# Where ScalarE copies the transposed rows of the second normalisation, and three waits at the end of an attention stage

## What is computed

```python
x = x + tanh(g_xattn[0]) * xattn(layernorm(x), ctx, ctx, mask, Wq, bq, Wk, bk, Wv, bv)
x = x + tanh(g_ffn[0]) * ffn(layernorm(x), Wg, W1, W2, W3)

# xattn: softmax over the 128 keys of the sequence
scores = einsum('bqhd,bkhd->bhqk', Qh, Kh) / sqrt(10.0)
scores = where(mask == 0, -1e9, scores)
out = einsum('bhqk,bkhd->bqhd', softmax(scores), Vh)

# ffn: every expert takes its top tokens
scores = (x_flat @ Wg.T).T
top_vals, token_idx = top_k(scores, capacity)
h = silu(xg @ W1.T) * (xg @ W3.T)
y = (h @ W2.T) * softmax(top_vals)[..., None]
out = zeros.at[token_idx].add(y)
```

## Time and profile before

| | us |
|---|---|
| median of 3 runs | 866.33 (866.3 to 868.46) |
| profiled execution, its own time | 867.74 |
| its span, first to last instruction | 866.0 |
| PE busy | 756.6 (87%) |
| DVE busy | 564.3 (65%) |
| ACT busy | 512.4 (59%) |
| POOL busy | 370.4 (43%) |

### The profile page before, as it was taken

How to read it: one execution, slowest core, us unless ns; L and a number is a source line. 1 busy time by engine, 2 the same in 40 slices (tenths; PEclk the granted TensorE clock), 3 DMA queues, 4 the chain that set the end, 5 groups by cost and what they waited for, 6 DMA issues and landing times. The chain is left out here.

```text
span 866.0 us, 24846 instructions
## 1 busy us (share of the span) xinstructions
PE 756.6 (87%) x9570; PEld 633.0 (73%) x9570; DVE 564.3 (65%) x1436; ACT 512.4 (59%) x1001; POOL 370.4 (43%) x777
## 2 busy tenths in 40 slices
PE   1599999999999999999998841599999999999993
PEld 1477878777877778777876720379888888988983
DVE  3367877777777777777776689755746556474440
ACT  3236676767766776677765757265555655556641
POOL 6232444424452435343522230435484654747505
PEclk9779999999999999999999975599999999999997
DMA  4243345335433544355312235135364453624314
GB/s 133 88 137 121 113 157 164 106 124 174 163 120 119 165 163 131 108 164 164 127 64 91 78 97 174 50 123 117 95 109 117 81 112 71 131 46 86 37 13 49
DMA packets 76773, 97.07 MB, mean 112 GB/s; under 512 B 8264, under 2 KB 55880, under 8 KB 76616
## 3 DMA queue, kind: packets, MB, share of 16 engines
q1 hardware_dynamic: 64368, 78.44, 28.2%
q0 software_dynamic: 12288, 17.05, 12.1%
HBM read 52.37 MB, written 25.72 MB: 90 GB/s over the span
## 5 line engine op out<-in xcount | busy, mean ns | idle before, releaser
L725 DVE TENSOR_REDUCE m_sb<-a_ps 128x4 f32<-128x512 f32 x256 | 164.7, 685 | 69.4 <-PE a_ps L1017 60.0
L559 ACT ACTIVATE p_t<-b_ps 128x512 f32<-128x512 f32 x252 | 141.6, 589 | 84.5 <-PE b_ps L1025 82.1
L1017 PE MATMUL a_ps<-k_st,q_st 31*128 31x128 f32 x2048 | 152.2, 287 | 10.6 <-DMA q_st<-q_val 5.9
L1017 PEld LDWEIGHTS a_ps<-k_st,q_st 31*128 31x128 f32 x2048 | 128.0, 190 | 36.3 <-issue 31.8
L1411 POOL DMA_INDIRECT out<-y,idx_add x64 | 100.3, 1567 | 110.7 <-ACT y L1470 100.0
L1025 PE MATMUL b_ps<-q_st,k_st 32*128 32x128 f32 x1984 | 144.4, 283 | 0.0
L475 POOL TENSOR_TENSOR x<-o_n,x_res 128x256 f32<-128x256 f32 x63 | 46.1, 731 | 208.2 <-DVE o_n L814 176.1
L1025 PEld LDWEIGHTS b_ps<-q_st,k_st 32*128 32x128 f32 x1984 | 120.7, 187 | 0.0
L1792 PE MATMUL bank<-x_hi,w_hi 128*128 128x512 f32 x254 | 100.0, 394 | 0.0
L1657 DVE TENSOR_TENSOR act_h<-act_h,bank 128x512 f32<-128x512 f32 x64 | 44.0, 688 | 84.4 <-PE bank L1792 78.3
L1792 PE MATMUL bank<-x_lo,w_hi 128*128 128x512 f32 x254 | 99.0, 390 | 0.0
(11 more groups left out here) (283 smaller groups left out, 1726.2 us busy)
## 6 DMA issues: line engine op xcount, KB each, us to landing
w<-in_w_t SPq DMA_DIRECT2D x24, 512.0 KB
rows_scratch<-xg SPq DMA_DIRECT2D x16, 528.0 KB, 3.5
x_in<-in_x SPq DMA_DIRECT2D x16, 512.0 KB, 4.7
c_t<-in_ctx_t SPq DMA_DIRECT2D x16, 512.0 KB, 4.6
k_st<-k_val SPq DMA_DIRECT2D x64, 128.0 KB
q_st<-q_val SPq DMA_DIRECT2D x64, 128.0 KB, 2.4
x_res<-in_x SPq DMA_DIRECT2D x16, 512.0 KB, 3.8
out<-x SPq DMA_DIRECT2D x16, 512.0 KB, 3.2
```

The source lines that it names most:

```text
L559: act.activation(p_t[b.s % 2][:, 4 * r:4 * r + 4, :], ps[q % 2][:].rearrange("p (h s) -> p h s", s=P), ACT.Exp, scale=SCALE).then_inc(exp_ ...
L725: dve.tensor_reduce(m_sb[b.s % 2][:, 4 * q:4 * q + 4], a_ps[q % 2][:].rearrange("p (h s) -> p h s", s=P), AX_X, ALU.max).then_inc(max_done, 1)
L1017: mm = pe.matmul(a_ps[i][:, t * P:(t + 1) * P], q_st[p][r:r + A_K, t, tok], k_st[p][r:r + A_K, t, tok], start=True, stop=True)
```

## The change

In ScalarE's `step` the copy `xt2_copy` moves ahead of the two first exponentials and the negated maximum. At the attention's end four things are done. PE's `values` of the last batch, which writes `f_ps`, no longer waits for ScalarE's copy out of `pv_ps` (`pv_out`) but for the second copy of transposed rows (`xt2_out`), which is the last reader of `f_ps`. `scores_back` moves ahead of `out_back(NB - 3)` and `values(NB - 2)` on PE. On VectorE `fold_last(1)` moves behind the division of batch NB-3, and the statistics of batches NB-3 and NB-2 change places with divisions. The scaled output of the last batch gets a tile of its own, `o_n_last`, so that it need not wait until GpSimd has read `o_n`.

```diff
+    o_n_last = sb("o_n_last", [P, D])
...
             def step(act, b):
                 g, f = b.group, b.group.on(1)
+                if b.j < 2:
+                    xt2_copy(g.on(-3), b.j)
                 exp(b.back(2), 0)
                 negate(b.back(1))
                 exp(b.back(2), 1)
-                if b.j < 2:
-                    xt2_copy(g.on(-3), b.j)
...
-            def scale_out(b, ps=o_ps):
+            def scale_out(b, ps=o_ps, to=o_n):
...
-                wait(dve, x2_done, b.times(1))
+                if to is o_n:
+                    wait(dve, x2_done, b.times(1))
...
-                dve.tensor_tensor(o_n[:].rearrange("p (h d) -> p h d", d=DH), o[:, :, 0:DH],
+                dve.tensor_tensor(to[:].rearrange("p (h d) -> p h d", d=DH), o[:, :, 0:DH],
...
             row_scores(group(NG - 3))
-            fold_last(1)
             divide(batch(NB - 3))
             scale_out(batch(NB - 3))
+            fold_last(1)
+            row_stats(batch(NB - 3))
             divide(batch(NB - 2))
-            row_stats(batch(NB - 3))
             scale_out(batch(NB - 2))
             divide(batch(NB - 1), b_ps[0])
+            scale_out(batch(NB - 1), b_ps[0], o_n_last)
             row_stats(batch(NB - 2))
-            scale_out(batch(NB - 1), b_ps[0])
             add_last()
...
-                    wait(pe, pv_out, b.times(1))
+                    if ps is pv_ps:
+                        wait(pe, pv_out, b.times(1))
+                    else:
+                        pe.wait_ge(xt2_out, back.times(2, 2))
...
+            scores_back(group(NG - 3), edge)
             out_back(batch(NB - 3))
             for q in range(4):
                 values(batch(NB - 2), q, group(NG - 3))
-            scores_back(group(NG - 3), edge)
             for q in range(4):
                 values(batch(NB - 1), q, group(NG - 3), f_ps)
```

More of the change, by code:

```diff
@@ L892, in add_last @@
                 dve.wait_ge(s_res[1], b.group.turn(16, 16))
-                dve.tensor_tensor(x2[1][:, b.j, :], o_n[:], x_res[1][:, b.j, :], ALU.add).then_inc(x2_done, 1)
+                dve.tensor_tensor(x2[1][:, b.j, :], o_n_last[:], x_res[1][:, b.j, :], ALU.add).then_inc(x2_done, 1)
             def last_scales():
```

## The result

The changed kernel takes 842.23 us (median of 4 runs, 841.49 to 843.42) where the kernel before takes 866.32. The ratio is 0.9717, with a 95% interval of 0.9698 to 0.9737. The profiled execution has its own time of 842.56 us and a span of 840.8 us; the forecast was 841.6 us and a span of 841.3.

A forecast was written before the change was run, and what follows sets the result against it. PE was taken to bound the kernel, busy 756.6 of 866.0 us, idling 20.5 us for ScalarE's copy. Gains of 18.5 + 4.5 + 1.7 = 24.7 us off 866.33 gave 841.6 us, range 839.5 to 846.5.

The forecast's parts named there:

- The steady groups: Twelve groups with copies: PE's wait ahead of values goes, 1.24 us in j=0 and 0.30 in j=1, 18.5 us in all.
- The cover: ScalarE ahead of the first exponential: the copy fits in idle time, with 0.53 us left in j=0.
- The margin at the step's end: End of steady step j=0: PE stays last, 0.16 us behind VectorE's chain (6.32 against 6.16 us).
- Rival (b): Steady step j=0: VectorE or ScalarE takes PE's place, 4.9 us lost, 846.5 us; chance 0.12.
- The last group: Final group with copies: two steps fall to 5.15 and 5.3 us, gaining 4.5 us, with PE's clock fall gone.
- rival (a): Final group with copies and attention's end give less, only 3.3 and 0.75 us: 843.8 us; chance 0.14.
- The end: Attention's end: three waits or delays on the chain to last_scales go, 1.7 us in all.
- PE's 0.75: Attention's end: values of the last batch starts earlier, no longer waiting for ScalarE's o_t, gaining 0.75 us.
- VectorE's two: Attention's end: statistics leave the way between division and scaling, 0.5 us; the wait for GpSimd's addition goes, 0.48 us.
- VectorE would wait for POOL nowhere: Attention's end, sign in the changed profile: VectorE has no wait for GpSimd (POOL).
- (c): PE ahead of values: the wait only changes its name, such as to the batch's exponentials; 860 us, chance 0.04.
- (d): Denser PE gets a lower clock: 7% lost eats the 24.7 us, 8% gives 871 us; chance 0.02.

The follow-up runs named there:

- second-place kernel: The changed kernel with ScalarE's copy one place further back, between the first exponential and the negated maximum; 851.87 us, ratio 0.9811.
- runs with more copies: The changed kernel with added ScalarE copies behind the moved one: 128x512, 128x1024 or both; 842.8, 843.2 and 850.1 us.
- kernel with the old last group: The changed kernel with ScalarE's copy back behind the exponentials in the final group that has copies only; 847.6 us, ratio 0.9769.
- PE's end alone: The changed kernel with VectorE's order and single o_n at the attention's end put back, PE's edits kept; 843.39 us in one execution.
- VectorE's end alone: The changed kernel with PE's edits at the attention's end put back, VectorE's edits kept; 845.9 us in one execution.
- the move alone: The kernel before with only ScalarE's copy moved ahead of the exponentials, nothing done at the attention's end; 844.39 us, ratio 0.974.

## Why the prediction was right

**The steady groups.** Predicted 12 x 1.54 = 18.5 us, measured 18.8. The step lengths were forecast as 6.32 and 7.42 us and came out as 6.32 and 7.39. What carried this was the group without copies, which runs the same steps with the same partners: it showed both where `values` can start and what would be last if it did. The second-place kernel shows the cause itself.

**The cover.** The copy was taken to lie in ScalarE's idle time with 0.53 us left; 0.60 us were. The margin at the step's end was given as 0.16 us and measured as 0.15. Rival (b) was priced at 0.41 us a step for a push of 0.57; the runs with more copies pay 0.05 for 0.21 and 0.57 for 0.72, the same line. Its mechanism was named too narrowly: PE's wait for the second exponential comes at the same delay as VectorE's chain, and PE meets it first.

**The last group.** Predicted 5.15 and 5.3 us, measured 5.11 and 5.29, and the gain of 4.5 us came out as 4.5. The step behind that number is sound only in part. The gain consists of 3.1 us that are always there (6.54 + 7.00 - 5.11 - 5.29) and of a fall of the clock, which cost 1.4 us in the one execution of the kernel before that was profiled (7.95 - 6.54) and 2.8 in an execution of the kernel with the old last group (7.73 + 8.62 - 6.54 - 7.01). I took one execution's fall as a property of the kernel. What the median holds of it these runs don't settle; in an execution without a fall rival (a) has this term nearly right, with 3.3 us for 3.1. The sum also took the gain from one base and set it against another: the profiled execution, with its fall of 1.4 us, lay 1.4 us above the median of 866.33, and all 24.7 us were taken off the median. Without the fall the terms are 18.8 + 3.1 + 1.6 = 23.5 us, which gives 842.8; measured were 24.1 and 842.2. That 841.6 came so near is in part luck. The Trainium skill, TensorE: Matmul & The Clock Gate, section on HAM oscillation, describes a loop in which waits for DMA, longer than the gaps here, bring the clock down each time round. Of eight gaps of 1.6 us here, three were followed by a fall, and of the last group's steps with a gap of 1.0 us or none no step had one: the falls came only with the longer idle time, but it did not bring one each time.

**The end.** Predicted 1.7 us, measured 1.57 up to `last_scales`. By terms: PE's 0.75 came out as 0.85. VectorE's two, 0.5 and 0.48, came out as 0.64 together when alone, and as 0.7 on top of PE's (1.57 - 0.85). In the changed kernel (DVE and POOL):

```profile
475.24 0.43 DVE L826 BATCH_NORM_STATS2 stats<-x 128x6 f32<-128x256 f32 x1 [0.64 <-POOL x L476]
...
477.06 0.26 DVE L804 RECIPROCAL rden<-b_ps 128x16 f32<-128x16 f32 x1
477.36 0.44 DVE L811 TENSOR_SCALAR rden_g<-rden,gx 128x16 f32<-128x16 f32 x1
477.83 0.42 DVE L816 TENSOR_TENSOR o_n_last<-b_ps,rden_g 128x256 f32<-128x256 f32 x1
```

```profile
477.04 0.72 POOL L476 TENSOR_TENSOR x<-o_n,x_res 128x256 f32<-128x256 f32 x1 [1.84 <-DVE o_n L816]
```

The scaling of the last batch now runs while GpSimd adds, and its small product `rden_g` takes 0.44 us, where it takes 0.20 in the kernel with PE's end alone: it ends at 477.80, just after GpSimd's addition at 477.76. So of the wait of 0.48 us that was to go, 0.2 came back. The sum came within 0.2 us because PE's term was 0.1 too small and VectorE's two 0.3 too large, which is luck in part. The forecast that VectorE would wait for POOL nowhere was wrong: its first statistics now wait 0.64 us for GpSimd's addition. That costs nothing here, since they are through at 475.88 and the division behind them, at 475.97, needs transposes of PE that end at 475.94.

**Rivals (c) and (d).** No wait took the place of the old one (0.0 us ahead of `values`), and the denser PE kept its clock:

```profile
120.00:440.00 320.00, 319.29 (x5723) 266.16 (x5727) 253.39 (x643) 235.61 (x480) 136.56 (x438) 1.00 0.45 146
```

PE is busy for 99.8% of this stretch at a clock of 1.00, where it was 94.7%. Waits of PE are worth no more than 0.7 us there now; what makes the steady steps shorter has to come from its work.

## What to carry to other kernels

Where a short copy is always ready and its reader always waits, look at what stands ahead of it in its own engine's queue; if that waits for something itself, the copy belongs in front. Before relying on it, find a stretch of the same trace that runs without the copy: it gives the gain, and the margin of what is late next. And where one step of many runs at a lower clock, look at a second execution before its cost goes into a sum.

## What the runs showed of the hardware

A fall of the clock behind idle time of PE isn't a property of the program. With 1.6 us idle in each of two steps, one kernel took 7.73 and 8.62 us in one execution and 6.54 and 7.01 in another, both with the same code. What decides between the two is open.

VectorE's small product of 128x16 for the last batch took 0.43 to 0.44 us in all ten traces with VectorE's new order, in which it ran beside GpSimd's addition (with VectorE's end alone it went from 481.26 to 481.70 and the addition from 480.94 to 481.66). It took 0.20 us in the three with the old order (the kernel before, the move alone, PE's end alone), where it came after the addition. All ten times it ended 0.02 to 0.04 us after the addition. The Trainium skill, SBUF — State Buffer, section "Who interferes with whom", describes a pair of ports that VectorE and GpSimd share under an exclusive lock; the rows agree with that. No run here was made to separate the two engines, so the cause is argued and not shown.
